# Power-attention layer on one core: who copies the weighted sums out of PSUM

## The chip, the cores and the metric

One program on one core of one Trainium2 chip. The metric is device time in microseconds (us) for one execution, from launch to end; a run's figure is the median of several executions. Engines are called by their profile names: PE (TensorE matmul), PEld (TensorE weight load), DVE (VectorE), ACT (ScalarE), POOL (GpSimd), SP (SyncE, which issues DMAs).

## The reference, cut to what matters

The program is a stack of four layers over x of 16 batches x 256 tokens x 128 channels, each with a layer norm before it, a layer norm after it and a residual sum: softmax attention, softmax attention with a mixture of experts, **power attention**, and a second mixture of experts with limited places. The change lies in the third:

```
q, k, v, gates = x @ W.T                       # 16 heads of 8 channels
log_G = cumsum(log_sigmoid(gates))             # decays
S = q k.T                                      # per head, 256 x 256
Z = 2*log(|S| + 1e-7) + log(scale) + log_G[t] - log_G[s],  s <= t only
P = exp(Z - rowmax(Z));  y = (P @ v) / sum(P)
x = x + layernorm(y)
```

exp of twice a logarithm is a square, so the kernel computes P as (|S| + 1e-7) squared times exp of the decays, without the maximum; numerator and denominator both come out of one product with V that has a column of ones.

## The kernel before, in words

The power layer (`power_layer`) works through 16 batches, called steps t. A step has 16 heads in 8 units u of two heads; n = 8t + u counts the units. Queries and keys are split in two halves of 128 tokens, so that each head has a near part (two diagonal blocks) and a far part (late queries against early keys). Each engine runs one hand-written loop over t and u, and the order in those loops is the order on the engine. For one unit:

- PE `near_blocks(n)` makes the decays (`decay_ps`, two buffers, line 1553) and the near scores (line 1557), one unit ahead; `far_scores(n)` (line 1571) the rest of the scores and so releases S. Ahead of the decays stands a mask matmul (line 1536); in steps below 10 one extra mask matmul, and in steps 14 and 15 two (line 1535), whose results are overwritten: filler.
- DVE takes |S| out of PSUM (line 1412, `AP`), a bit mask on integers, as the first work of its slot n.
- ACT makes exp of the decays (line 1232, `EP`) in slot n and the square of |S| (line 1220, `PTP`) of unit n - 1.
- POOL multiplies the two (line 991) in its slot n + 2.
- PE `times_v(t, g)` (line 1590) takes four heads (group g of 4) at once: 24 matmul records into one PSUM bank `pvP`, 384 columns. Its places are u = 6 of step t and u = 0, 2, 4 of step t + 1.
- `sums(t, g)` copies this bank to `OSP` in SBUF. The bank is single: `times_v` of the next group waits for the copy (`s_os`). The slots of the copies are u = 7 of step t and u = 1, 3, 4 of step t + 1; in slot 4 the product stands in the same unit of PE.
- In u = 5, 6, 7 of step t + 1 PE turns the sums (`turn_out`, line 1509, needs all four copies), and DVE divides them (`far_sums` L1330, `normalize_early`, `normalize_late` L1337).

S and |S| lock into each other: PE's `far_scores(n)` waits for |S| of n - 1, DVE's |S| of n waits for `far_scores(n)`; |S| has four buffers, freed by the squares. PE's mask matmul of n + 1 waits for ACT's exponential of n - 1.

Between these stand the small works of other batches. On ACT: `turned_in` (L1108, yT, slot 3; PE's projection L1468 of the same unit waits for it), `in_root` (slot 3), `out_root` (L1174 lvP and L1176 prsP, slot 4), `high` (L1112 HLP, slot 4; DVE's `low_parts` L1273 in slot 5 wait for it), `values` and `softplus` (slot 7; DVE's `log_gates` of slot 7 wait for them), and in slot 7 of steps 3, 6 and 9 rows of the layer before. On DVE: moments, decay rows, `far_keys` (slot 6), and guests of the layer before in steps 3, 6 and 9 (L2556 and others).

Of the kernel before, what the change touches and what calls it, by code (L numbers as in the profile page):

```python
# [36 lines left out]
ACT = mybir.ActivationFunctionType  # L37
# [3 lines left out]
P = 128  # L41
# [5 lines left out]
NG, NJ = 4, 4  # L47
# [783 lines left out]
def power_layer(nc, low, weighted_in, top, take, X, cst, cstb, QK, Vx, w, Y, chosen, router, bias, yd, wi, wo, gated, dram):  # L831
# [6 lines left out]
    UNITS = gated.UNITS  # L838
    with ExitStack() as ctx:
# [4 lines left out]
        def pb(name, banks):  # L844
            return ctx.enter_context(nc.psum_tensor(f"{name}P", [P, banks, 512], F32))

        def sem(name):
            return take(f"{name}P")
# [4 lines left out]
        pv_ps = pb("pv", 1)  # L853
# [20 lines left out]
        OS = sb("OS", [P, 2, 3, NG, P], F32)  # L874
# [18 lines left out]
        full = {n: sem(f"full_{n}") for n in POWER_A + POWER_B}  # L893
# [18 lines left out]
        s_pv = sem("s_pv")  # L912
        s_os = sem("s_os")
# [20 lines left out]
        def has(t):  # L934
            return 0 <= t < NB
# [29 lines left out]
        def reach(eng, sem, count):  # L965
            if count > 0:
                eng.wait_ge(sem, count)
# [180 lines left out]
        def scalar(act, guests):  # L1148
            def values(t):
                reach(act, full["V"], t + 1)  # L1150
                reach(act, free["V"], t)
                wide = bank("V").rearrange("p (c s) -> p c s", c=TC)
                act.activation(ge[:], wide[:, :, D:D + H], ACT.Abs).then_inc(s_ge, 1)
                reach(act, s_pv, NG * (t - 2))
                act.activation(Vx[:, t % 3, :, :, 0:DH], wide[:, :, 0:D].rearrange("p c (h d) -> p c h d", d=DH),
                               ACT.Copy).then_inc(s_ge, 1)

            def softplus(t):
                act.wait_ge(s_ge, 4 * t + 2)
                act.activation(ge[:], ge[:], ACT.Exp, scale=-1.0).then_inc(s_ge, 1)  # L1160
                act.wait_ge(s_ge, 4 * t + 3)
                act.activation(ge[:], ge[:], ACT.Ln, bias=1.0).then_inc(s_ge, 1)

            def in_root(t):
                act.wait_ge(s_ln, 4 * t + 4)
                reach(act, s_y, 2 * t)
                act.activation(lv[:, 0, :], mv[:, :, 1], ACT.Ln, bias=eps[:, 1:2]).then_inc(s_rs, 1)
                act.wait_ge(s_rs, 2 * t + 1)
                act.activation(rs[:], lv[:, 0, :], ACT.Exp, scale=-0.5).then_inc(s_rs, 1)

            def out_root(t):
                act.wait_ge(s_lp, 4 * t + 4)
                reach(act, s_tmp, 2 * t)
                act.activation(lv[:, 1, :], pmv[:, :, 1], ACT.Ln, bias=eps[:, 1:2]).then_inc(s_prs, 1)  # L1174
                act.wait_ge(s_prs, 2 * t + 1)
                act.activation(prs[:], lv[:, 1, :], ACT.Exp, scale=-0.5).then_inc(s_prs, 1)  # L1176

            def factors(t):
                reach(act, full["CS"], t + 1)
                reach(act, s_yn, t - 2)  # L1180
                act.activation(fac[:, t % 3, :, :], bank("CS")[:, S:S + 2 * H].rearrange("p (a h) -> p a h", a=2),
                               ACT.Exp).then_inc(s_fac, 1)

            def route_root(t):
                act.wait_ge(s_rl, 4 * t + 4)
                reach(act, s_Y, t)
                act.activation(rlv[:], rmv[:, :, 1], ACT.Ln, bias=eps[:, 1:2]).then_inc(s_rrs, 1)
                act.wait_ge(s_rrs, 2 * t + 1)
                act.activation(rrs[:], rlv[:], ACT.Exp, scale=-0.5).then_inc(s_rrs, 1)

            def route_norm(t):
                act.wait_ge(s_rnm, t + 1)
                for c in range(TC):
                    last = act.activation(Y[:, t * TC + c, :], batch_rows(t)[c], ACT.Identity, bias=rnm[:, c:c + 1],
                                          scale=rrs[:, c:c + 1])
                last.then_inc(s_Y, 1)

            def route_turned(t):
                act.wait_ge(full["RT"], t + 1)
                reach(act, full["RL"], t)  # L1200
                act.activation(YT[:], bank("RT")[:, 0:S], ACT.Copy).then_inc(free["RT"], 1)

            def odds():
                act.wait_ge(s_choose, 2)
                act.activation(chosen.ex[:, 0:EARLY, :], chosen.pr[:, 0:EARLY, :], ACT.Exp).then_inc(s_odds, 1)

            def second_odds():
                act.wait_ge(s_choose, 8)
                act.activation(chosen.gap[:, 0:EARLY], chosen.gap[:, 0:EARLY], ACT.Exp).then_inc(s_odds, 1)

            def square(n):
                act.wait_ge(s_abs, n + 1)
                reach(act, s_pv, (n - NW) // 2 + 1)
                if n == 5:
                    act.wait_ge(gated.s_up, UNITS)
                if n == 8:
                    gated.stores(act, 1)
                if n == 9:
                    act.wait_ge(gated.s_sum, 2 * gated.EARLY)
                act.activation(PT[:, n % NW, :], A[:, n % NA, :], ACT.Square, bias=eps[:, 0:1]).then_inc(s_sq, 1)  # L1220

            act.preload_act_table_set("natural_log_exp_and_others")
            act.wait_ge(s_zero, 3)
            for t in STEPS:
                for u in range(NU):
                    n = NU * t + u
                    if has(t):
                        act.wait_ge(s_decay, n + 1)
                        weighted(act, n - NE)
                        if n == 0:  # L1230
                            act.wait_ge(gated.s_prod, UNITS)
                        act.activation(E[:, n % NE, :], decay_ps[:, n % 2, :], ACT.Exp).then_inc(s_taken, 1)  # L1232
                    if 0 <= n - 1 < NU * NB:
                        square(n - 1)
                    if u == 4 and has(t - 2):
                        out_root(t - 2)
                    if u == 3 and has(t + 2):
                        turned_in(act, t + 2)
                    if u == 2 and t >= EARLY_CS - 1 and has(t + 1):
                        factors(t + 1)  # L1240
                    if u == 2 and t >= EARLY_CS - 1 and has(t + 1):
                        first_part(act, t + 1)
                    if u == 4 and has(t + 2):
                        high(act, t + 2)
                    if u == 3 and has(t + 3):
                        in_root(t + 3)
                    if u == 7 and has(t + 2):
                        values(t + 2)
                    if u == 7 and has(t + 2):
                        softplus(t + 2)  # L1250
                    for b in due("route_turned", t, u):
                        route_turned(b)
                    for b in due("route_root", t, u):
                        route_root(b)
                    for b in due("route_norm", t, u):
                        route_norm(b)
                    if t == NB and u == 5:
                        odds()
                    if t == NB + 1 and u == 5:
                        second_odds()  # L1260
                    guests.get((t, u), nobody)()
# [38 lines left out]
        def vector(dve, guests):  # L1300
            def log_gates(t):
# [1 line left out]
                reach(dve, full["CS"], t)  # L1303
                x = bank("V").rearrange("p (c s) -> p c s", c=TC)[:, :, D:D + H]
                dve.scalar_tensor_tensor(lg[:], x, 0.0, ge[:], ALU.min, ALU.subtract).then_inc(free["V"], 1)

            def sums(t, g):
                if t == 0 and g == 0:
                    dve.wait_ge(gated.s_down, UNITS)
                reach(dve, s_pv, NG * t + g + 1)  # L1310
                reach(dve, full["OT1"], t - 1)
                dve.tensor_copy(OS[:, t % 2, :, g, :], pv_ps[:, 0, 0:3 * P].rearrange("p (a s) -> p a s", a=3)).then_inc(s_os, 1)

            def far_keys(t):
                dve.wait_ge(s_fac, t + 1)
# [88 lines left out]
            for t in STEPS:  # L1404
                for u in range(NU):
                    n = NU * t + u
                    if has(t):
                        dve.wait_ge(s_S, n + 1)
                        reach(dve, s_sq, n - NA + 1)
                        if n == 3:  # L1410
                            dve.wait_ge(gated.s_down, UNITS)
                        dve.tensor_scalar(A[:, n % NA, :].bitcast(I32), score_ps[:, n % 2 * WU:n % 2 * WU + WU].bitcast(I32),  # L1412
                                          0x7FFFFFFF, None, ALU.bitwise_and).then_inc(s_abs, 1)
                    if u == 7 and has(t):
                        sums(t, 0)
                    if u == 1 and has(t - 1):
                        sums(t - 1, 1)
                    if u == 3 and has(t - 1):
                        sums(t - 1, 2)
                    if u == 4 and has(t - 1):  # L1420
                        sums(t - 1, 3)
                    if 0 <= n - 2 < NU * NB and (n - 2) % NU in MULT_BY_DVE:
                        multiply(dve, n - 2)
                    if u == 0 and has(t - 2):
# [1730 lines left out]
```

## Time and profile before

| | us |
|---|---|
| median of 3 runs (lowest, highest) | 1150.97 (1149.85, 1159.54) |
| the profiled execution | 1146.26 |
| its span, first to last instruction | 1144.5 |
| busy in the span: PE / DVE / ACT / POOL | 1006.8 / 880.9 / 767.3 / 692.8 |
| power layer, first to last step | 688.2 to 993.6 of the span |

Busy time is the time in which an engine had an instruction running; PE's ends are modelled, so its share says little. In the rows below a time in front of an engine's name is the start from the span's start; the next number is the duration of the instruction or of several merged ones; brackets at the end give the idle time of the engine in front and what ended it.

### The profile page before, as it was taken

The numbers are of one execution on the slowest core, as the hardware profiler recorded it, in microseconds if no ns is written. First come the engines' busy times: TensorE is split into PE (matmuls) and PEld (weight loads), VectorE is DVE, ScalarE is ACT, GpSimd is POOL, SyncE is SP. The second block draws the span as 40 slices with busy tenths as digits, with TensorE's granted clock in tenths as the row PEclk, the third lists the DMA queues.
The fourth block names the chain that finished last, engine by engine and source line by source line (L and its number), as shares of the span: only waits on it lengthen the run. The fifth ranks groups of instructions, "written<-read, shape, count | busy, mean of one in ns | idle before, by whom it ended". The sixth has DMA issues, their size and how long they took to land. (4 is left out here: it accounts for less than half of the span.)

```text
span 1144.5 us, 30966 instructions
## 1 busy us (share of the span) xinstructions
PE 1006.8 (88%) x10503; PEld 591.1 (52%) x10503; DVE 880.9 (77%) x2252; ACT 767.3 (67%) x1682; POOL 692.8 (61%) x814
## 2 busy tenths in 40 slices
PE   4899999999999977998999978989899999828975
PEld 2344444444444433457998854545455565524652
DVE  3899999999998996946657638989998999873323
ACT  1678888888888865873545646868687898743315
POOL 4244554566566538842776536878886887725763
PEclk9999999999999998989999988979897999957997
DMA  4112222211111111212534311112120112141227
GB/s 128 30 58 79 76 71 74 74 57 39 39 39 39 40 33 49 60 41 63 156 102 128 105 48 27 45 38 61 42 66 24 34 45 65 36 165 34 54 69 196
DMA packets 114423, 75.24 MB, mean 66 GB/s; under 512 B 21335, under 2 KB 107808, under 8 KB 114272
## 3 DMA queue, kind: packets, MB, share of 16 engines
q1 hardware_dynamic: 105840, 54.68, 17.5%
q0 software_dynamic: 7744, 18.13, 5.3%
q8 instruction: 90, 1.47, 0.5%
q14 instruction: 61, 0.50, 0.1%
q10 hardware_dynamic: 688, 0.46, 0.1%
HBM read 26.75 MB, written 26.51 MB: 47 GB/s over the span
## 5 line engine op out<-in xcount | busy, mean ns | idle before, releaser
L634 DVE TENSOR_REDUCE mxsS<-scoreS 128x2 f32<-128x512 f32 x512 | 327.4, 684 | 46.3 <-PE scoreS L776 42.5
L516 ACT ACTIVATE PTS<-stS 128x512 f32<-128x512 f32 x512 | 284.6, 596 | 62.0 <-PE stS L780 61.5
L776 PE MATMUL scoreS<-QK 31*128 31x256 f16 x1024 | 172.0, 280 | 29.0 <-DVE mxsS L634 16.5
L991 POOL TENSOR_TENSOR PTP<-PTP,EP 128x512 f32<-128x512 f32 x128 | 163.0, 1285 | 50.7 <-ACT PTP L1220 50.2
L780 PE MATMUL stS<-QK 32*128 32x256 f16 x1024 | 169.3, 277 | 1.3 <-ACT PTS L516 1.3
L698 PE MATMUL pvS<-PTS,Vx 128*32 128x256 f32 x2048 | 141.2, 394 | 0.3
L1220 ACT ACTIVATE PTP<-AP,epsP 128x768 f32<-128x768 f32 x128 | 119.1, 931 | 28.5 <-DVE AP L1412 28.2
L776 PEld LDWEIGHTS scoreS<-QK 31*128 31x128 f16 x1024 | 52.9, 93 | 151.0 <-DVE mxsS L634 104.4
L1412 DVE TENSOR_SCALAR AP<-score_psP 128x768 int32<-128x768 int32 x128 | 121.4, 949 | 12.3 <-PE score_psP L1571 11.3
L391 POOL TENSOR_TENSOR rsS<-veS,halfS 128x2 f32<-128x2 f32 (+1 forms) x32 | 33.1, 1035 | 134.4 <-DVE veS L602 67.9
L1232 ACT ACTIVATE EP<-decay_psP 128x512 f32<-128x512 f32 x128 | 75.8, 592 | 29.7 <-PE decay_psP L1553 28.4
L2170 POOL DMA_INDIRECT sorted<-gy,gidx x64 | 62.1, 971 | 37.2 <-DVE gowner L2511 18.6
L698 PEld LDWEIGHTS pvS<-PTS,Vx 128*32 128x32 f32 x2048 | 54.3, 111 | 50.3 <-issue 22.7
L2309 PE MATMUL gdown_ps<-down_w,gprod 128*128 (+1 forms) x496 | 65.7, 276 | 4.4 <-DVE XB L2545 4.4
L2309 PEld LDWEIGHTS gdown_ps<-down_w,gprod 128*128 128x128 f32 x496 | 60.3, 192 | 5.9 <-issue 4.9
L2599 DVE TENSOR_TENSOR gprod<-gsg,gup_ps 128x512 f32<-128x512 f32 x62 | 42.5, 686 | 21.7 <-PE gup_ps L2337 12.6
L2181 POOL DMA_INDIRECT ggot<-mixed,gidx x40 | 39.1, 977 | 32.8 <-DMA mixed<-gob 22.0
L1553 PEld LDWEIGHTS decay_psP<-MP 32*128 32x128 bf16 x512 | 29.6, 95 | 52.7 <-issue 48.2
L2358 ACT ACTIVATE ghTs<-gturn_ps,norm 128x256 f16<-128x256 f32 x46 | 21.7, 472 | 51.6 <-PE gturn_ps L2248 51.6
L780 PEld LDWEIGHTS stS<-QK 32*128 32x128 f16 x1024 | 52.2, 92 | 4.6 <-ACT PTS L516 2.4
L1571 PE MATMUL score_psP<-QK 31*128 31x128 f16 x256 | 37.1, 226 | 19.6 <-DVE AP L1412 19.0
L1557 PE MATMUL score_psP<-QK 31*128 31x128 f16 x512 | 52.5, 224 | 0.0
(397 smaller groups left out, 2415.6 us busy)
## 6 DMA issues: line engine op xcount, KB each, us to landing
QK<-HLS SPq DMA_DIRECT2D x384, 32.0 KB
QK<-HLP SPq DMA_DIRECT2D x192, 32.0 KB, 1.9
gsin<-sorted SPq DMA_DIRECT2D x46, 128.0 KB
mixed<-gob SPq DMA_DIRECT2D x46, 128.0 KB, 1.8
sorted<-ggot POOLq DMA_DIRECT2D x22, 256.0 KB, 2.6
expert_outputs<-tzero SPq DMA_DIRECT2D x8, 512.0 KB
cgot<-expert_outputs SPq DMA_DIRECT2D x16, 256.0 KB, 5.4
tokens<-XB SPq DMA_DIRECT2D x16, 128.0 KB, 3.0
```

The lines of the kernel that those rows point to most:

```text
L516: act.activation(PT[:, n % NPT, :], st_ps[:, (NS * t + n) % 3, :], ACT.Exp, scale=SCALE).then_inc(s_exp, 1)
L634: dve.tensor_reduce(mxs[:, u // 4, :, at], score_ps[:, n % 2, :].rearrange("p (c s) -> p c s", c=TC), AX.X, ALU.max).then_inc(s_max, 1)
L698: last = pe.matmul(pv_ps[32 * j:32 * j + 32, q], Vx[:, t % 3, c, 4 * g + j, :], PT[:, (4 * g + (j ^ 2)) % NPT, S * c:S * c + S], start=(c ...
L776: scored = pe.matmul(score_ps[:, k, cols], QK[part, new, g, 0, rows], QK[part, new, g, 1, :], start=True, stop=True)
L780: turned = pe.matmul(st_ps[:, (NS * t + n) % 3, cols], QK[part, old, g, 1, rows], QK[part, old, g, 0, :], start=True, stop=True)
L991: eng.tensor_tensor(w, w, E[:, n % NE, :], ALU.mult).then_inc(s_wd if n % NU in MULT_BY_DVE else s_wp, 1)
L1220: act.activation(PT[:, n % NW, :], A[:, n % NA, :], ACT.Square, bias=eps[:, 0:1]).then_inc(s_sq, 1)
L1232: act.activation(E[:, n % NE, :], decay_ps[:, n % 2, :], ACT.Exp).then_inc(s_taken, 1)
L1412: dve.tensor_scalar(A[:, n % NA, :].bitcast(I32), score_ps[:, n % 2 * WU:n % 2 * WU + WU].bitcast(I32), 0x7FFFFFFF, None, ALU.bitwise_and) ...
L1557: pe.matmul(score_ps[:, o:o + P], QK[band, t % 3, g, 1, rows], QK[band, t % 3, g, 0, rows], start=True, stop=True)
L2170: pool.indirect_dma_start(tables[h], bass.IndirectOffsetOnAxis(ap=idx[h][:, c, t:t + 1], axis=0), y[:, tiles[h].start + t, :], None).then_ ...
L2309: last = pe.matmul(down_ps[:, x % 2, t * D:(t + 1) * D], prod[:, x % NPROD, c * SLOTS + t * P:c * SLOTS + (t + 1) * P], down_flat[:, colum ...
```

## The change

The four copies of a step (`sums`) leave DVE's loop and enter ACT's loop, in slots of the same number. On DVE a copy stood right behind |S|; on ACT it stands behind the exponential and the square of the slot, ahead of `out_root`, `turned_in`, `high`, `values` and `softplus`. Waits and the count of `s_os` are the same; the instruction is an activation with the function Copy.

```diff
@@ scalar(act): new @@
+            def sums(t, g):
+                if t == 0 and g == 0:
+                    act.wait_ge(gated.s_down, UNITS)
+                reach(act, s_pv, NG * t + g + 1)
+                reach(act, full["OT1"], t - 1)
+                act.activation(OS[:, t % 2, :, g, :], pv_ps[:, 0, 0:3 * P].rearrange("p (a s) -> p a s", a=3), ACT.Copy)\
+                   .then_inc(s_os, 1)
...
                     if 0 <= n - 1 < NU * NB:
                         square(n - 1)
+                    if u == 7 and has(t):
+                        sums(t, 0)
+                    if u == 1 and has(t - 1):
+                        sums(t - 1, 1)
+                    if u == 3 and has(t - 1):
+                        sums(t - 1, 2)
+                    if u == 4 and has(t - 1):
+                        sums(t - 1, 3)
                     if u == 4 and has(t - 2):
                         out_root(t - 2)
                     if u == 3 and has(t + 2):
                         turned_in(act, t + 2)
@@ vector(dve, guests): taken out @@
-            def sums(t, g):
-                if t == 0 and g == 0:
-                    dve.wait_ge(gated.s_down, UNITS)
-                reach(dve, s_pv, NG * t + g + 1)
-                reach(dve, full["OT1"], t - 1)
-                dve.tensor_copy(OS[:, t % 2, :, g, :], pv_ps[:, 0, 0:3 * P].rearrange("p (a s) -> p a s", a=3)).then_inc(s_os, 1)
...
-                    if u == 7 and has(t):
-                        sums(t, 0)
-                    if u == 1 and has(t - 1):
-                        sums(t - 1, 1)
-                    if u == 3 and has(t - 1):
-                        sums(t - 1, 2)
-                    if u == 4 and has(t - 1):
-                        sums(t - 1, 3)
```

## Rows read from the trace of the kernel before

**Rows 1.** Busy windows: whole stage; columns are stretch, length, engines' busy us, clock
```profile
688.22:993.60 305.38, 284.02 (x3486) 159.22 (x3484) 277.65 (x625) 239.89 (x501) 242.49 (x223) 0.93 0.17 43
```
**Rows 2.** The same by step: 3, 4, 5, 6, 8, then 10 to 13 together, 11
```profile
743.87:770.40 26.53, 21.82 (x223) 11.30 (x222) 23.14 (x56) 15.44 (x34) 18.45 (x18) 0.74 0.13 34
770.40:789.35 18.95, 18.07 (x229) 10.11 (x229) 18.07 (x40) 16.69 (x38) 17.26 (x17) 1.00 0.24 58
789.35:808.00 18.65, 17.96 (x229) 10.10 (x228) 17.81 (x39) 15.29 (x34) 16.97 (x17) 1.00 0.22 58
808.00:832.11 24.11, 19.99 (x229) 10.89 (x228) 23.03 (x57) 15.59 (x35) 18.46 (x18) 0.86 0.17 43
851.05:873.04 21.99, 20.62 (x229) 11.27 (x228) 17.93 (x40) 15.65 (x34) 15.67 (x15) 0.84 0.17 41
895.62:960.85 65.23, 64.55 (x883) 40.00 (x883) 61.54 (x150) 61.33 (x135) 55.17 (x51) 1.00 0.17 46
912.23:928.27 16.04, 15.94 (x221) 9.95 (x220) 15.31 (x39) 15.13 (x35) 14.13 (x15) 1.00 0.14 35
```
**Rows 3.** Waits, stage and its tail: who waited for whom, total us, times, longest
```profile
PE score_psP L1571 <- DVE AP L1412: 19.0, 20, 3.9
DVE OSP L1312 <- PE pvP L1590: 11.2, 15, 2.0
```
**Rows 4.** Timeline of PE: first and last of the five longest such waits
```profile
704.61 0.28 PE L1571 MATMUL score_psP<-QK 31*128 31x128 f16 x2 [3.87 <-DVE AP L1412]
...
878.59 0.28 PE L1571 MATMUL score_psP<-QK 31*128 31x128 f16 x2 [0.74 <-DVE AP L1412]
```
**Rows 5.** Waits in steps 10 to 13
```profile
PEld score_psP L1571 <- DVE AP L1412: 3.1, 10, 0.6
...
ACT EP L1232 <- PE decay_psP L1553: 1.5, 3, 0.6
ACT lvP L1167 <- DVE mvP L1269: 1.4, 3, 0.7
```
**Rows 6.** Instruction groups of the stage: busy us, mean ns, idle before and releaser
```profile
L1312 DVE COPY OSP<-pvP 128x384 f32<-128x384 f32 x64 | 35.1, 548 | 12.0 <-PE pvP L1590 11.2 <-DVE pr L161 0.8
```
**Rows 7.** Instruction groups of ACT, same columns
```profile
L1232 ACT ACTIVATE EP<-decay_psP 128x512 f32<-128x512 f32 x128 | 75.8, 592 | 29.7 <-PE decay_psP L1553 28.4 <-POOL PTP L991 1.0
L1108 ACT ACTIVATE yTP<-misc_aP 128x256 f32<-128x256 f32 x14 | 5.2, 369 | 0.0
```
**Rows 8.** Timeline of ACT in step 11, slots 3 and 4
```profile
918.78 0.37 ACT L1108 ACTIVATE yTP<-misc_aP 128x256 f32<-128x256 f32 x1
...
921.74 0.28 ACT L1174 ACTIVATE lvP<-pmvP,epsP 128x2 f32<-128x2 f32 x1
...
922.16 0.58 ACT L1112 ACTIVATE HLP<-misc_aP 128x512 f16<-128x512 f32 x1
922.64 0.59 ACT L1232 ACTIVATE EP<-decay_psP 128x512 f32<-128x512 f32 x1
```
**Rows 9.** Timeline of PE in step 11, same slots
```profile
919.39 0.70 PE L1468 MATMUL misc_aP<-yTP,wq 128*128 128x256 f32 x2
...
921.78 0.40 PE L1590 MATMUL pvP<-PTP,VkP 128*32 128x128 f32 x8
```
**Rows 10.** Timeline of DVE in step 11, the copy of slot 4
```profile
922.25 0.56 DVE L1312 COPY OSP<-pvP 128x384 f32<-128x384 f32 x1 [0.45 <-PE pvP L1590]
```
**Rows 11.** Waits in steps 4 and 5
```profile
PEld score_psP L1571 <- DVE AP L1412: 2.8, 8, 0.4
...
PEld score_psP L1571 <- issue: 1.6, 8, 0.2
```
**Rows 12.** Timeline of DVE in step 6: the copy of slot 4
```profile
824.25 0.56 DVE L1312 COPY OSP<-pvP 128x384 f32<-128x384 f32 x1 [0.71 <-PE pvP L1590]
```
**Rows 13.** Timeline of PE in step 6: the scores of unit 6
```profile
827.13 0.28 PE L1571 MATMUL score_psP<-QK 31*128 31x128 f16 x2 [1.28 <-DVE AP L1412]
```
**Rows 14.** DVE's normalize line: count, then min/median/max ns, first and last start
```profile
L1337 DVE TENSOR_TENSOR ynP<-farP,rcP x16: 291/680/3061, 727.2 to 1002.7; 128x128 f32<-128x128 f32 x16
```

## The prediction

> **What bounds the kernel now.** The page's busy shares, in the table above, show no engine but PE near full over the whole program, and PE's share is no limit by itself, since its ends are modelled. So I cut out the one stage that the change touches. Its sixteen steps take 305 us; DVE is busy 278 of them, ACT 240 [rows 1], and DVE looks like the bound. By steps (a stretch runs from the first |S| of a batch on DVE to that of the next) there are three kinds [rows 2]. Steps 4 and 5 (2 and 7 are their like) take 18.95 and 18.65 us at full clock, PE busy 18. Steps 10 to 13, without the filler matmul, take 65.2 us or 16.3 each; in step 11 PE, DVE and ACT are all within 0.9 of the length. Steps 3, 6 and 8 (9 is their like) take 22 to 26.5 with the granted clock at 0.74 to 0.86 on average: partly 1.2 instead of 2.4 GHz.
>
> Who waits for whom decides whether DVE is the bound. PE's score matmuls wait 19.0 us for |S| in the whole stage, in 20 places [rows 3]. The five longest, in time order 3.87, 3.66, 2.84, 1.37 and 0.74 (first and last in [rows 4]), make 12.5 of it. One lies in step 0 behind DVE's guest work, four in steps 3, 6, 8 and 9 behind DVE's slot 0, in which no copy of sums stands. In steps 10 to 13 all waits of PE's weight loads for |S| are 3.1 us, 0.8 a step [rows 5]. So DVE is nearly full, yet frees PE in time: S, |S| and the next S go at PE's pace, and each DVE slot has only to fit into one PE unit.
>
> **The change part by part.** *Off DVE:* 64 copies of 0.548 us, 35.1 us, and the 11.2 us that DVE idles in front of them for the product with V [rows 6, 3]. *Onto ACT:* 64 copies of 128x384 out of PSUM. No ACT instruction of that shape is in the trace; its neighbours take 0.369 us (128x256) and 0.592 (128x512), both PSUM to SBUF [rows 7], so 0.48 by interpolation, with those two as bounds. Back to back ACT overlaps by 0.10: HLP starts at 922.16 and takes 0.58, its follower starts at 922.64 [rows 8]. So a copy occupies ACT for 0.38 us (0.27 to 0.49), 1.5 us a step.
>
> *The wait that moves with it.* Three of the four slots mostly find the product done; the copy in slot 4 doesn't, and DVE idles 0.45 us for it in step 11 [rows 10]. On ACT it stands behind the square that ends by 921.74 and ahead of lv/prs and HLP [rows 8]. The product with V ends at 921.78+0.40=922.18 [rows 9]: ACT would sit about 0.45 us. It becomes a little more. The copy of slot 3 is now ahead of yT, which ends at 918.78+0.37=919.15 [rows 8]; PE's projection starts 0.24 later [rows 9] and stands ahead of the product in PE's queue, so 0.38 more before yT makes it 0.1 to 0.3 late when ACT has no slack. I take 0.55 for the wait, bounds 0.3 and 0.8. Queued behind it on ACT are prs, HLP and the exponentials of the decays; DVE's low parts wait for HLP, PE's mask matmuls for the exponentials.
>
> *Steps 10 to 13.* ACT is busy 61.3 of 65.2 us [rows 2]. Add 16 copies of 0.38 (6.1) and four waits of 0.55 (2.2): 69.6. The 3.9 us that ACT idles now are mostly 1.5 for decays and 1.4 for moments [rows 5]; both end because ACT arrives later, so they are filled first. ACT becomes the bound, 69.6 against 65.2; of the 4.4 some 0.4 are absorbed by PE being one unit ahead at the end: **+4.0**. Bounds: +2 (no wait, all idle filled) and +8 (the idle stays).
>
> *Steps 2, 4, 5, 7.* PE's floor is close: in steps 4 and 5 its weight loads wait 2.8 us for |S| in 8 places, but a usual pause there is 1.6/8=0.2 [rows 11], so 0.6 a step is over. Of that the copies make a part, above all the one in slot 1, which delays |S| 2 and 3: 0.3 a step comes back. Against it stands ACT. In step 5 it is busy 15.29 of 18.65 [rows 2], and 1.5+0.55 fit, though HLP comes some 0.8 later and takes back what DVE gained in slot 4. In step 4 it is busy 16.69 of 18.95, with rows of the layer before; 16.69+1.5+0.55=18.74 leaves nothing, and yT and HLP make PE wait. I take -0.3 for steps 2 and 5, +0.4 for 4 and 7: **+0.2**; bounds -2 (all of the 0.6 comes back, less a little) and +3 (0.8 lost in each).
>
> *Steps 3, 6, 9.* In slot 4 of step 6 DVE does the copy after a wait of 0.71 [rows 12], then guest moments, then |S| 5, and PE waits 1.28 us for that |S| [rows 13]. Wait and copy, 0.71+0.55, leave DVE's path: -1.1 in each of three steps. But ACT enters the next step (4, 7, 10) with as much work on a shorter time, and gives back about 0.8 each: **-0.9** together; bounds -4 and 0. The stall of slot 0 has no copy in it and stays, and with it the low clock.
>
> *Steps 0, 1, 8, 14, 15 and the tail:* PE is the bound there (at the low clock, or with two fillers); ACT has idle time there, and in the tail it is mostly waiting. That idle time hides the copies; without it they would cost up to 1.5 us a step in steps 14 and 15: **-0.1**.
>
> Sum: 4.0+0.2-0.9-0.1 = **+3.2 us** on the profiled execution's 1146.26 (1144.5 span and 1.8 around it): 1149.5. The runs shown lie at 1149.85 to 1159.54 with a median of 1150.97, 4.7 above the profiled one. The time asked for is such a median, so 1150.97+3.2: **1154**. A measurement of this kernel tells 1% (11.5 us) from no change.
>
> **The rivals.** *DVE is the bound.* For: 278 of 305 us busy, the fullest of DVE, ACT and POOL; a full removal would be 35.1+11.2=46 us less, 1105 [rows 1, 3, 6]. Against: PE hardly waits. Of the 19.0 us of PE's waits 19.0-12.5=6.5 lie outside the five stalls [rows 3, 4]: -6.5, **1144.5**, chance 0.13; the full 46 us get 0.02. The Trainium skill, page Perfetto Trace Analysis, section Identifying Performance Opportunities, says to relieve the engine with the highest occupancy and not to trust TensorE's matmul busy share. By that rule the change gains, towards this rival's 1105, where the sum by waits loses 3.2 us. The trace agrees only as far as the occupancy goes, 278 us against 240; its waits speak the other way.
>
> *The clock falls less.* For: DVE's normalize instruction on two SBUF operands takes 0.29 to 3.06 us for one shape [rows 14], and the longest stands in step 8, while POOL multiplies back to back; with squares coming later from ACT the multiplies separate, DVE gets in between, and the falls in steps 8 and 9 go. Each costs about 3 us (step 8: 21.99 against 18.65 of step 5 [rows 2]). Two fewer, with some slot 0 time: -9, **1145**, chance 0.12. Against: POOL has a backlog in slot 0, so a square 0.8 later is still in time. The Trainium skill's page SBUF — State Buffer, section Who interferes with whom, describes an exclusive lock between VectorE and GpSimd for operations with two SBUF inputs; the 0.29 to 3.06 us agree with it.
>
> *ACT is the bound everywhere* (slower). Mechanism: the wait in slot 4 blocks HLP and the exponentials in steps with a filler too, DVE's low parts and PE's decays wait on ACT, and PE loses 0.8 to 1 us in each of steps 2 to 9 as well. It decides from the point where ACT's busy time, copies and wait exceed the step: 18.74 against 18.95 in step 4. Price 8x0.9+4.0, with nothing gained in 3, 6, 9: +11, **1162**; new idle stretches of PE could add a clock fall of 3 us. Chance 0.16.
>
> That the change doesn't do what it says: the copies are plainly ACT's in the diff; 0.02, then 1151.
>
> **How the numbers follow.** Forecast 0.55, around 1154 from 1148 to 1160; DVE bound 0.15; clock 0.12; ACT everywhere 0.16; no change 0.02. The range takes in the bounds of the sum and reaches past the middles of the moderate rivals on both sides, which leaves out some 0.2: 1142 to 1164. Faster by over 1% (below 1139.5): the full DVE case, and part of the two moderate ones if they come together, 0.07. Slower by over 1% (above 1162.5): the upper half of ACT everywhere and a little of the forecast, 0.11. The rest, 0.82, lies within.
>
> **What would show it.** Right: steps 10 to 13 at about 17.1 us each with ACT busy over 16.5 and DVE about 13.5; ACT idle before the slot-4 copy for V's product by about 0.5 us in each step; PE's projection or decays waiting for ACT where nothing waits now; steps 3 and 6 still with a fallen clock; DVE idle several us more in total. The copy at 0.45 to 0.50 us. Wrong: steps 10 to 13 as short as before (then ACT's idle holds more than I think), steps 4, 5, 7 below 18 us (then PE did wait on DVE), or a changed count of stretches at half clock, which moves the time by 3 us each and which no sum of busy times foresees.

## The result and the profile after

The changed kernel takes 1169.63 us (median of 4 runs, 1166.56 to 1172.84) beside 1150.41 for the kernel before (4 runs, 1145.11 to 1159.54): a ratio of **1.0162, 95% interval 1.0110 to 1.0214**. It is slower, and lies above the predicted range. The profiled execution took 1171.17 us (span 1169.3). The ratios here and below leave out executions more than 1.5% above the fastest of the same kernel.

First the busy windows of the changed kernel, with the columns of [rows 1, 2]: the whole stage, steps 1, 3, 4, 6, 7, 9, 10, and 11 to 13 together; then three short stretches.

```profile
691.90:1016.71 324.81, 296.08 (x3484) 164.59 (x3482) 260.88 (x565) 258.51 (x562) 242.09 (x223) 0.89 0.16 41
711.62:730.84 19.22, 17.94 (x213) 9.71 (x209) 15.97 (x33) 15.38 (x34) 14.05 (x13) 0.90 0.10 25
749.71:773.35 23.64, 19.34 (x223) 10.23 (x222) 21.50 (x53) 15.78 (x35) 17.63 (x17) 0.86 0.15 40
773.35:795.90 22.55, 20.95 (x229) 11.45 (x228) 17.30 (x37) 18.20 (x42) 18.05 (x18) 0.85 0.20 47
814.68:838.25 23.57, 20.10 (x229) 10.84 (x228) 21.49 (x53) 16.78 (x38) 17.62 (x17) 0.86 0.18 46
838.26:860.81 22.55, 20.95 (x229) 11.44 (x228) 17.31 (x37) 18.20 (x42) 18.04 (x18) 0.85 0.20 48
883.69:907.35 23.66, 22.07 (x230) 11.69 (x230) 19.72 (x53) 16.79 (x38) 14.53 (x14) 0.78 0.10 26
907.35:932.29 24.94, 23.17 (x221) 13.62 (x220) 15.25 (x36) 18.27 (x43) 16.06 (x16) 0.66 0.11 30
932.29:983.96 51.67, 48.71 (x663) 30.09 (x663) 42.10 (x98) 48.57 (x110) 39.87 (x37) 1.00 0.16 43
774.90:780.50 5.60, 4.12 (x44) 2.17 (x36) 5.57 (x13) 5.04 (x10) 5.19 (x5) 1.00 0.50 114
780.50:787.30 6.80, 6.80 (x53) 3.53 (x52) 3.94 (x10) 4.97 (x13) 5.36 (x6) 0.50 0.05 12
913.60:930.70 17.10, 17.10 (x147) 9.79 (x145) 9.12 (x19) 10.49 (x24) 10.82 (x11) 0.50 0.07 17
```

The same windows of the kernel before, as far as the rows ahead don't have them: steps 1, 7, 9, 10, then 11 to 13, and the part of step 4 that answers to 774.90:780.50.

```profile
707.80:725.67 17.87, 17.87 (x217) 9.84 (x214) 16.38 (x37) 14.54 (x30) 14.39 (x13) 0.89 0.09 23
832.11:851.05 18.94, 18.07 (x229) 10.10 (x229) 18.07 (x40) 16.70 (x38) 17.25 (x17) 1.00 0.23 58
873.04:895.62 22.58, 20.56 (x228) 11.32 (x227) 20.70 (x56) 15.63 (x34) 14.56 (x15) 0.85 0.10 27
895.62:912.23 16.61, 16.23 (x221) 10.02 (x220) 15.95 (x41) 15.66 (x36) 12.98 (x12) 1.00 0.14 37
912.23:960.85 48.62, 48.32 (x663) 29.98 (x663) 45.59 (x111) 45.67 (x100) 42.18 (x40) 1.00 0.18 49
771.95:777.55 5.60, 5.28 (x76) 3.06 (x70) 5.57 (x15) 4.47 (x10) 5.00 (x5) 1.00 0.47 111
```

The stage is 324.81-305.38=19.4 us longer. The stage also starts 3.7 us later, which no edit explains (its start scatters from 685.6 to 691.9 over the kernels of this study), and the rest is behind it. Read the clock column against [rows 2]. Steps 4 and 7 ran at 1.00 (2.4 GHz); now they hold a stretch at 0.50 (1.2 GHz) and take 22.55 us each, +3.60 and +3.61. Step 10 has a stretch of 17.1 us at 0.50 and goes from 16.61 to 24.94, +8.3. These three make 15.5 of the 19.4. Steps 11 to 13 stay at full clock and take 51.67 instead of 48.62, +3.05. Each kernel has one trace, while the mean clock differs from execution to execution (0.921 to 0.931 in the four of the changed kernel); so the steps are read from one pair of traces, and the verdicts further down go by the times of many executions.

The windows of 5.60 us show what came ahead of the fall: in this stretch of step 4 PE was busy 5.28 us before and 4.12 after, and then the clock falls for 6.8 us. Length times one minus the clock estimates what a stretch loses: 305.38x0.07=21.4 us before, 324.81x0.11=35.7 after. So some 14 of the 19.4 us are clock (1.6 either way, from the rounding of each clock), and the work at full clock grew by about 5.

Who makes PE idle in step 4 is in its timeline (changed kernel; in brackets the idle time before, and its releaser):

```profile
776.05 0.39 PE L1536 MATMUL decay_psP<-cstb 128*128 128x512 bf16 x1 [0.52 <-ACT EP L1240]
...
778.91 0.58 PE L1522 MATMUL misc_aP<-router,YTP 128*128 128x8 f32 x4 [0.62 <-ACT YTP L1209]
779.83 0.28 PE L1572 MATMUL score_psP<-QK 31*128 31x128 f16 x2 [0.34 <-DVE AP L1421]
```

Twice the profile names ACT: the exponential of the decays and the turned rows of the route (YT) are late. The third wait is DVE's, whose normalize row of slot 0 now meets POOL's multiplication (775.47 to 776.75). It is shown as it was in the kernel before, and as it is now, with the |S| that PE waits for:

```profile
771.90 0.49 DVE L1337 TENSOR_TENSOR ynP<-farP,rcP 128x128 f32<-128x128 f32 x1
```
```profile
774.83 2.08 DVE L1346 TENSOR_TENSOR ynP<-farP,rcP 128x128 f32<-128x128 f32 x1
...
778.82 0.96 DVE L1421 TENSOR_SCALAR AP<-score_psP 128x768 int32<-128x768 int32 x1
```

DVE was busy without a gap up to this |S|, and PE's scores start as it ends. Had YT come in time, PE would have stood for |S| all the same: of the 1.48 us in step 4 only the first 0.52 are ACT's by the wait that ends last, the other 0.96 are DVE's. Step 7 repeats this (0.52, 0.63 and 0.33). Step 10 has 0.41, 0.52 and 0.84 us for ACT and none for DVE there.

The copies, and ACT's exponentials (groups of the stage; a few records are missing):

```profile
L1240 ACT ACTIVATE EP<-decay_psP 128x512 f32<-128x512 f32 x127 | 75.1, 591 | 9.5 <-PE decay_psP L1554 8.2 <-POOL PTP L991 1.0
L1189 ACT ACTIVATE OSP<-pvP 128x384 f32<-128x384 f32 x61 | 29.8, 488 | 30.1 <-PE pvP L1591 30.1
```

A copy takes 0.488 us. ACT used to idle 29.7 us in front of its exponentials [rows 7]; that was its lead over PE. Now it idles 9.5 there and 30.1 in front of the copies, with the exponentials behind. Slot 4 of step 11 and of step 10, on ACT:

```profile
941.29 0.93 ACT L1228 ACTIVATE PTP<-AP,epsP 128x768 f32<-128x768 f32 x1
942.65 0.49 ACT L1189 ACTIVATE OSP<-pvP 128x384 f32<-128x384 f32 x1 [0.43 <-PE pvP L1591]
...
943.94 0.59 ACT L1240 ACTIVATE EP<-decay_psP 128x512 f32<-128x512 f32 x1
...
923.17 0.49 ACT L1189 ACTIVATE OSP<-pvP 128x384 f32<-128x384 f32 x1 [3.34 <-PE pvP L1591]
```

In steps in which no fall begins (1, 2, 5 and 11 to 15) this wait is 0.42 to 1.24 us; in step 11 it is 0.43. In step 10, inside the stretch at 0.50, PE reaches the product late and ACT stands 3.34 us for it; in steps 4, 7, 8 and 9, in a low stretch or right behind it, 2.5 to 3.3. So in these steps the low clock comes with a longer wait, and the wait stands ahead of what PE needs next.

### The profile page after: what moved, and what is told of

Read it like the earlier page. It is cut to its first block and busy times, and to the rows that moved or that the text cites. A ratio compares the mean times of both kernels' runs of the same rounds, so it can differ in the third digit from the quotient of the medians.

```text
span 1169.3 us, 30967 instructions
## 1 busy us (share of the span) xinstructions
PE 1024.0 (88%) x10503; PEld 599.9 (51%) x10503; DVE 862.5 (74%) x2188; ACT 788.7 (67%) x1746; POOL 694.0 (59%) x814
## 3 DMA queue, kind: packets, MB, share of 16 engines
q1 hardware_dynamic: 105840, 54.68, 17.2%
## 5 line engine op out<-in xcount | busy, mean ns | idle before, releaser
L1228 ACT ACTIVATE PTP<-AP,epsP 128x768 f32<-128x768 f32 x128 | 119.4, 933 | 21.6 <-DVE AP L1421 21.4
L1537 PE MATMUL decay_psP<-cstb 128*128 128x512 bf16 x128 | 53.6, 419 | 1.5 <-ACT EP L1240 1.5
L1189 ACT ACTIVATE OSP<-pvP 128x384 f32<-128x384 f32 x64 | 31.3, 489 | 34.6 <-PE pvP L1591 34.6
```

The lines of the kernel that those rows point to most:

```text
L1537: pe.matmul(decay_ps[:, n % 2, :], cstb[:, 0:P], late, start=True, stop=False)
```

## The experiments

The theories that the expectations name: **A**, the copies of slots 7 and 1 behind the guest's rows on ACT; **B**, ACT is too full, and every copy costs the same; **C**, the copy of slot 4 (or 3 and 4), which waits ahead of ACT's small works and exponentials; **D**, late squares push POOL's multiplications onto DVE's instruction of slot 0; **E**, PE is stopped by ACT directly; **F**, the three slot-4 copies of steps 3, 6 and 9. All ratios are to the kernel before, timed beside it; brackets are 95% intervals. A split keeps the deleted copy on DVE for the slots that the test leaves there.

**Which slots.** In these a test goes in front of each call; `g` is the slot's number (0 to 3 for slots 7, 1, 3, 4):

```diff
+        def on_act(t, g):
+            return g in (0, 1)            # slots71;  g in (2, 3): slots34;  g == 3: s4only
-                    if u == 4 and has(t - 1):
+                    if u == 4 and has(t - 1) and on_act(t - 1, 3):
                         sums(t - 1, 3)
```

> The copies of slots 7 and 1 are ACT's, those of slots 3 and 4 stay DVE's. Theory A (two copies in slots 7 and 1, behind the guest rows that ACT does in slot 7 of steps 3, 6 and 9, make ACT late in units 0 and 1 of steps 4, 7 and 10; PE waits there and its clock falls): the three steps stay near 22.5, 22.5 and over 20 us with a mean clock under 0.9, ratio to before 1.008 to 1.015. Theory B (ACT is simply too full, each copy costs the same wherever it stands): half of the change's loss, 1.008, spread over all steps. Theory C (the wait in slot 4 does it): 1.000 to 1.002, no new stretch at the low clock.

> The copies of slots 3 and 4 are ACT's, those of slots 7 and 1 stay DVE's. A: steps 4 and 7 stay at full clock and near 19 us, steps 11 to 13 at 16.5 to 17; ratio 1.000 to 1.004. B: 1.008. C: most of the loss, 1.012 to 1.016, with the clock falling in steps 4, 7 and 10.

> Only the copy of slot 4 on ACT, the other three on DVE as before. It is the one that sits waiting for V's product ahead of the exponentials. If that wait is what counts (theory C in its narrow form): most of the loss of the two copies of slots 3 and 4 together (1.0145), so 1.009 to 1.014. If the copy of slot 3 ahead of yT counts as much, or both only add up to the lateness that moves POOL: 1.000 to 1.006.

Slots 7 and 1 alone: 1.0038 [1.0002, 1.0073]. Slots 3 and 4: 1.0145 [1.0088, 1.0202]. Slot 4 alone: **1.0193 [1.0131, 1.0254]**. One of the four copies carries the whole loss, so B falls. In the profile of slot 4 alone, steps 4, 7 and 10 are long with a fallen clock as in the changed kernel:

```profile
771.84:796.99 25.15, 21.33 (x229) 11.47 (x229) 20.43 (x39) 17.07 (x39) 17.73 (x18) 0.80 0.18 43
839.43:863.37 23.94, 20.14 (x229) 10.85 (x229) 20.42 (x38) 17.06 (x39) 17.74 (x18) 0.86 0.18 45
909.46:931.48 22.02, 20.66 (x221) 12.16 (x220) 16.62 (x39) 16.72 (x39) 14.49 (x15) 0.77 0.11 28
```

But PE's waits there are not those of the changed kernel. In step 4 PE waits 0.15 and 0.25 us for ACT and then 3.29 for an |S| that DVE holds back behind its normalize row (step 7: 3.28, behind a row of 3.31):

```profile
773.33 3.33 DVE L1359 TENSOR_TENSOR ynP<-farP,rcP 128x128 f32<-128x128 f32 x1
```
```profile
780.55 0.39 PE L1593 MATMUL score_psP<-QK 31*128 31x128 f16 x2 [3.29 <-DVE AP L1434]
```

POOL multiplies meanwhile (774.00 to 776.50). So with this copy alone PE's waits in steps 4 and 7 are mostly those of D, and only in step 10 those of E (0.52 and 0.47 us for ACT). Nor do these three steps mark the loss by themselves: they are long in the one trace of `slots71` too (21.64, 21.65 and 22.00 us), whose time is within 0.4% of the kernel before.

**Sparing the guest's steps.** All on ACT but slot 7 of steps 3, 6 and 9 and slot 1 of the step behind: the same test with `(t, g) not in ((3, 0), (3, 1), (6, 0), (6, 1), (9, 0), (9, 1))`.

> As the changed kernel, but six copies stay DVE's: slot 7 of steps 3, 6 and 9, and slot 1 of the steps after them. A: the falls of the clock in steps 4, 7 and 10 are gone, these take about 19, 19 and 17.5 us, steps 11 to 13 still 17.1 to 17.3; ratio 1.002 to 1.006. B and C: 58 of 64 copies are still ACT's, so 1.013 to 1.016.

1.0190 [1.0137, 1.0243], no better than the change. A falls.

**The order on ACT.** All four calls go behind the small works of their slot (yT, lv/prs, the high parts, softplus, the route's rows); `s4late` does so with the copy of slot 4 alone on ACT:

```diff
-                    if u == 4 and has(t - 1):
-                        sums(t - 1, 3)
                     if u == 4 and has(t - 2):
                         out_root(t - 2)
...
                     for b in due("route_norm", t, u):
                         route_norm(b)
+                    if u == 4 and has(t - 1):
+                        sums(t - 1, 3)
```

> All four copies are ACT's in the same slots, but behind the slot's small works (yT, HLP, softplus, the turned route rows) instead of ahead of them. A: PE gets the turned route rows of unit 1 earlier, but the exponential of unit 0 is as late as in the change, so falls in steps 4, 7 and 10 become fewer but not all go; 1.005 to 1.012. B: as the change, 1.014 to 1.018. C: HLP and yT no longer wait for the product with V, so most of the loss is gone, 1.000 to 1.004.

> Only the copy of slot 4 on ACT, and behind the slot's small works (lv/prs, the high parts) instead of ahead of them: those run while V's product is still on its way, and the copy finds it done. If ACT's standing for the product is what makes the squares late: the loss of 1.0193 goes to 1.000 to 1.005. If it is that DVE no longer stands there and PE runs ahead, or the copy's 0.4 us on ACT: 1.010 to 1.018.

All four late: 1.0030 [0.9994, 1.0067]. Slot 4 late: **0.9999 [0.9966, 1.0032]**, against 1.0193 ahead of the same works. Copy, engine and what DVE is relieved of are the same; only the order differs, and the loss is gone. The times say so, not the traces: those of `late` and `s4late` are of long executions (1158.95, median 1157.80; 1158.49, median 1150.94), and steps 4, 7 and 10 have falls in them too. Step 4 of `s4late`:

```profile
769.40:798.13 28.73, 25.47 (x229) 13.50 (x228) 19.43 (x39) 17.43 (x39) 19.52 (x19) 0.64 0.16 45
```

Slot 4 of step 12 on ACT, at full clock, first in `s4only`, then in `s4late`:

```profile
956.93 0.92 ACT L1234 ACTIVATE PTP<-AP,epsP 128x768 f32<-128x768 f32 x1
958.33 0.49 ACT L1195 ACTIVATE OSP<-pvP 128x384 f32<-128x384 f32 x1 [0.47 <-PE pvP L1612]
...
959.14 0.58 ACT L1118 ACTIVATE HLP<-misc_aP 128x512 f16<-128x512 f32 x1
959.62 0.59 ACT L1246 ACTIVATE EP<-decay_psP 128x512 f32<-128x512 f32 x1
```

```profile
949.47 0.93 ACT L1234 ACTIVATE PTP<-AP,epsP 128x768 f32<-128x768 f32 x1
...
950.72 0.58 ACT L1118 ACTIVATE HLP<-misc_aP 128x512 f16<-128x512 f32 x1
951.20 0.48 ACT L1195 ACTIVATE OSP<-pvP 128x384 f32<-128x384 f32 x1
951.57 0.60 ACT L1246 ACTIVATE EP<-decay_psP 128x512 f32<-128x512 f32 x1
```

From the end of the square to the exponential: 959.62-957.85=1.77 us, and 951.57-950.40=1.17. In the kernel before it is 922.64-921.84=0.80 [rows 8 and the line below], in the changed kernel 943.94-942.22=1.72. Late, the copy finds its product done, because the high parts ran while it was on its way. The square of the kernel before:

```profile
920.91 0.93 ACT L1220 ACTIVATE PTP<-AP,epsP 128x768 f32<-128x768 f32 x1
```

**Wait or release?** ACT's wait for the product added to the kernel before, in slot 4 of every step (`wait_all`) or of steps 3, 6 and 9 (`wait_only`), all copies on DVE; and DVE's copy moved behind |S| of slot 5, ACT untouched (`dve_slot5`):

```diff
+                    if u == 4 and has(t - 1):          # wait_only: t in (3, 6, 9)
+                        reach(act, s_pv, NG * t)
                     if u == 4 and has(t - 2):
                         out_root(t - 2)
```
```diff
-                    if u == 4 and has(t - 1):          # dve_slot5, in DVE's loop
+                    if u == 5 and has(t - 1):
                         sums(t - 1, 3)
```

> The kernel before, all copies on DVE, with only ACT's wait for V's product added in slot 4 of every step. If the wait is enough: 1.010 to 1.018. If it needs DVE's release at the same place, as with the wait in steps 3, 6 and 9 alone (0.9995): 0.999 to 1.004.

> The kernel before, all copies on DVE, and only the wait of ACT added: in slot 4 of steps 3, 6 and 9 ACT waits for V's product before it goes on, as it would for a copy. If ACT's wait in front of the exponentials is the cause by itself: 1.008 to 1.018. If it takes DVE's release too (with DVE standing at the same place, PE does not run ahead and ACT has the 1.3 us after the product to catch up): 0.999 to 1.004.

> The kernel before, with DVE's copy of slot 4 moved behind |S| of slot 5, still on DVE: DVE's wait for V's product goes, and ACT gets nothing to do. If the release of DVE by itself is the cause, since PE then runs ahead of ACT: 1.005 to 1.015. If ACT's wait is needed: PE's waits of about 1.1 to 1.3 us in steps 3, 6 and 9 go and nothing takes their place, 0.992 to 1.000.

The wait alone in all steps: 1.0030 [0.9994, 1.0066]; in three steps: 0.9995 [0.9969, 1.0020]. DVE's release alone: 1.0049 [1.0013, 1.0086], though not cleanly, for PE's transposes now wait for the moved copy (1.24 us in step 3 of its profile). Neither gives 1.6%, nor do both together by addition. `s4late` has DVE's release and the copy's time on ACT, but no wait ahead of the small works, and loses nothing (0.9999). So the wait is needed, but not enough by itself; whether the release or the copy's time ahead of the small works has to go with it was not run. A reading that fits, though argued and not shown: in the kernel before DVE stands at the same product, holds |S| back there, and so PE can't run ahead of an ACT that waits.

**The three copies of steps 3, 6 and 9.** The test of the first group with `(t, g) in ((2, 3), (5, 3), (8, 3))`, the product's own `t` being one less (`only369`), and with `not in` (`guard369`).

> The kernel before with three of the 64 copies on ACT: those of slot 4 in steps 3, 6 and 9. In these steps DVE used to stand 0.7 us for V's product and hold back |S| 5 by the copy and the guest's moments. Theory F (with DVE let go, units 5 to 7 run ahead while ACT waits for the product in front of the exponentials; the guest's rows keep ACT from catching up, the squares and POOL's multiplications enter the next step 1 us late, DVE's additions of slot 0 collide with them, PE idles and the clock falls in steps 4, 7 and 10): 1.009 to 1.019 of the kernel before, from three instructions. If the lateness is piled up over all steps by every slot-4 copy: 0.999 to 1.004.

> All copies on ACT but these three, which DVE keeps. Theory F: steps 4, 7 and 10 without their new clock falls, or with one of three, and what is left is the 1 us each of steps 10 to 13: 1.002 to 1.007 of the kernel before. If every slot-4 copy counts: 1.012 to 1.017.

These three alone: 1.0057 [1.0026, 1.0088]. All but them: 1.0169 [1.0112, 1.0227]. F falls as the sole cause. In the profile of `guard369` step 4 is whole again, and the clock falls in steps 5, 7 and 10 (and in others):

```profile
772.78:791.88 19.10, 18.05 (x229) 10.18 (x229) 15.48 (x35) 17.63 (x41) 16.57 (x16) 1.00 0.21 56
791.88:813.58 21.70, 20.78 (x229) 11.35 (x228) 16.41 (x35) 16.68 (x38) 17.09 (x17) 0.84 0.21 49
838.24:860.08 21.84, 20.90 (x229) 11.29 (x229) 15.48 (x36) 17.75 (x41) 16.59 (x16) 0.84 0.19 50
908.69:931.43 22.74, 20.99 (x229) 12.45 (x228) 14.66 (x35) 17.84 (x42) 13.28 (x13) 0.77 0.10 27
```

**The clock.** More filler matmuls in the changed kernel, in the units where PE idled:

```diff
+    MORE = [(t, u) for t in (4, 7, 10) for u in (0, 1, 2)]
-                for _ in range(AGAIN if t >= NB - 2 else t < 10):
+                for _ in range(AGAIN if t >= NB - 2 else 3 if (t, u) in MORE else t < 10):
```

> The changed kernel with two more filler matmuls in each of units 0 to 2 of steps 4 and 7, and three in those of step 10 (0.2 us each at full clock, 4.5 us in all if none of it lies in an idle gap). If the loss is the clock that falls after the idle gaps of PE there: the falls in steps 4, 7 and 10 go, those steps come down to 19 to 20 us, and the time is 1.003 to 1.010 of the kernel before. If the loss is the waiting itself and the low clock would do no harm without it: the fillers come on top, 1.016 to 1.021.

1.0045 [1.0002, 1.0087] instead of 1.0162: work added, time saved. Steps 4, 7 and 10 of its profile:

```profile
776.51:795.28 18.77, 18.64 (x233) 10.49 (x233) 15.02 (x36) 17.19 (x40) 14.71 (x15) 1.00 0.16 44
842.22:861.52 19.30, 18.82 (x233) 10.55 (x232) 16.82 (x36) 17.70 (x41) 17.73 (x17) 1.00 0.22 56
906.94:925.35 18.41, 17.84 (x235) 10.66 (x234) 14.89 (x36) 17.54 (x41) 14.26 (x14) 1.00 0.12 32
```

All three at full clock: 18.77, 19.30 and 18.41 us with two or three fillers more in each of three units. ACT carries the same work as in the changed kernel; PE, slowed by the fillers, hardly waits for it there (0.23 and 0.34 us in step 10), and the clock stays. It isn't a clean test of E in step 4, for DVE's normalize row takes 0.29 us there and not 2.08. And this execution, at 1164.14 us the longest of five (median 1156.85), has falls elsewhere, in steps 3, 5 and 8 above all (27.64, 23.11 and 24.12 us). Step 3:

```profile
748.87:776.51 27.64, 24.63 (x225) 13.02 (x224) 21.03 (x52) 16.72 (x37) 18.20 (x17) 0.69 0.14 35
```

What the clock cost can be estimated over all executions, as the record has the span and the mean granted clock of each: span times one minus the clock, as a mean of the executions that the ratios use. It is 66.4 to 70.1 us in four series of the kernel before, timed beside the tests, 85.0 in the changed kernel, 86.8 with the copy of slot 4 alone, 69.5 with that copy late and 67.9 with the fillers. The rest of the span is 1078.6 to 1080.3 us before, 1082.9 in the changed kernel and 1081.6 with the copy of slot 4 alone. So most of the loss of these two was the clock's.

What sets off a fall isn't shown. Here is step 4 of `slots71`, a stretch and the one right behind it, and the same stretch of step 4 in `guard369`:

```profile
770.90:776.50 5.60, 4.81 (x58) 2.57 (x48) 4.45 (x14) 5.39 (x12) 3.97 (x5) 1.00 0.41 109
776.50:783.30 6.80, 6.80 (x51) 3.26 (x52) 4.49 (x11) 4.68 (x12) 6.19 (x6) 0.50 0.07 18
```
```profile
774.41:780.01 5.60, 4.80 (x58) 2.56 (x46) 4.44 (x14) 5.39 (x12) 3.97 (x5) 1.00 0.39 107
```

PE waits 0.17 and 0.63 us for ACT in both; the clock falls behind the first and stays at 1.00 behind the second. Short waits go ahead of the falls, but they don't bring one each time.

**The collision in slot 0.** The far sums are added in place in PSUM, and the normalize row has one operand there (the semaphores `s_far` and `free["OT1"]` take over):

```diff
-                dve.tensor_tensor(far[:], turned("OT1", t)[:, :, 0:DH + 1], far[:], ALU.add).then_inc(free["OT1"], 1)
+                dve.tensor_tensor(turned("OT1", t)[:, :, 0:DH + 1], turned("OT1", t)[:, :, 0:DH + 1], far[:], ALU.add)\
+                   .then_inc(s_far, 1)
-                divide(t, 1, far[:], s_yn)
+                divide(t, 1, turned("OT1", t), free["OT1"])
```

> The changed kernel with one edit: the far sums of slot 0 are added in place in PSUM, so that DVE's normalize multiplication has one operand in PSUM instead of two in SBUF. Theory D (the loss runs through POOL: ACT's squares come later, POOL's multiplications slide onto DVE's two-SBUF-operand multiplication in slot 0 of a step, which then takes 2.1 us in step 4 instead of 0.5; PE waits and the clock falls): that row falls to about 0.3 us in every step, slot 0 of steps 4 and 7 is 1 us shorter or more, at least two of the new clock falls go, 1.003 to 1.009 of the kernel before. Theory E (PE is stopped by ACT directly, by late exponentials and late yT, and the collision only happens beside it): slot 0 shrinks on DVE, PE's falls stay, 1.013 to 1.017.

> The kernel before with the same in-place addition in PSUM. Theory D: the stalls of slot 0 in steps 8 and 9, where that multiplication takes up to 3.06 us, shrink as well and one or two of the clock falls go: 0.985 to 0.997. Theory E, or if the guest's own instructions of slot 0 simply take the collision over: 0.998 to 1.002.

> All four copies on ACT behind the small works of their slots, and the far sums added in place in PSUM. If the two effects add up (1.0030 and the 0.9939 of the addition alone): 0.994 to 0.999, no better than the kernel before with the addition alone. If ACT in the better order lets DVE use what the addition frees: 0.986 to 0.992, the best version so far.

In the changed kernel: 1.0136 [1.0106, 1.0167]. In the kernel before: **0.9939 [0.9903, 0.9975]**. With all copies late on ACT: 0.9954 [0.9927, 0.9981]. The group of DVE's normalize rows, first of the kernel before, then of the changed kernel, then of the changed kernel with this edit:

```profile
L1337 DVE TENSOR_TENSOR ynP<-farP,rcP 128x128 f32<-128x128 f32 x14 | 15.6, 1112 | 0.5
```
```profile
L1346 DVE TENSOR_TENSOR ynP<-farP,rcP 128x128 f32<-128x128 f32 x14 | 20.5, 1466 | 0.5
```
```profile
L1346 DVE TENSOR_TENSOR ynP<-misc_bP,rcP 128x128 f32<-128x128 f32 x29 | 8.4, 291 | 1.0
```

The row costs 0.291 us wherever it stands. The Trainium skill, page SBUF — State Buffer, section Who interferes with whom, has an instruction of VectorE with two SBUF inputs contend with one of GpSimd that reads SBUF, and one with at most one (outside the two-port modes) not; these rows agree. The edit takes 0.6% off the kernel before. Off the changed one it takes nothing that can be told from no change (1.0136 beside 1.0162, with overlapping intervals), and the two with the edit lie 1.0136/0.9939=1.020 apart: the collision of this row is real, and the changed kernel's loss doesn't need it. In its trace (1154.98 us, the shortest of six, median 1161.66) PE waits 0.52 and 0.63 us for ACT in steps 4 and 7 as before, but not for DVE behind them, and both steps take 20.64 us, with the clock at 0.92 and 1.00; step 10 keeps its waits for ACT and its 24.93 us at 0.66. So E holds in step 10, and in steps 4 and 7 both play. `s4only`, where D is the larger part of the waits, was not run with this edit. Both kernels are beaten by `before_far`; the copies on ACT, in their better order, add nothing to it (0.9954).

## Why the prediction was wrong, step by step

**What bounds the kernel** was right as far as the copies go: taking them off DVE gained nothing, neither two of the slots (1.0038) nor all four with the better order on ACT (1.0030). The rivals with DVE as the bound (1144.5, 1105) fall with that. The list of PE's "five longest" waits is wrong, though (so is the title of [rows 4]): two of 1.28 us and one of 1.05, in steps 6, 9 and 3 behind the copy of slot 4, are longer than the 0.74. And DVE's slot 0, which holds no copy, does bind: its normalize row was worth 0.6% (`before_far`).

**The copy** was 0.48 us by interpolation, measured 0.488. **The wait in slot 4** was 0.55 us, measured 0.43 in step 11. For the whole stage the same number would make 9 us; ACT idled 30.1 in front of the copies, most of it in or behind low stretches. The square before it ends at 921.84 and not by 921.74, which is small beside that.

**Steps 10 to 13** were +4.0, as 17.1 us a step. Steps 11 to 13 came as forecast: 51.67/3=17.2 each, +3.05, with ACT at 16.2 busy (over 16.5 was the sign) and DVE at 14.0 (about 13.5). Step 10 did not: +8.3, with 17.1 us at the low clock, for which the sum has no term.

**Steps 2, 4, 5, 7, the failed step.** The prediction says: "In step 4 it is busy 16.69 of 18.95 [...] leaves nothing, and yT and HLP make PE wait. I take [...] +0.4 for 4 and 7". That ACT without slack makes PE wait holds in part: PE waited for the exponential and YT rather than yT and HLP, and behind them for an |S| of DVE's that the term doesn't have. The size is wrong. Measured: +3.60 and +3.61; steps 2 and 5 have +0.67 and +0.12 where -0.3 each was forecast. The waits were priced as their own length, 0.4 us a step. They were 1.48 us, and behind them 6.8 us ran at 1.2 GHz, some 3.4 us lost. With fillers the same steps take 18.77 and 19.30 us at full clock. The upper bound (0.8 us lost in each) left the clock out as well.

**Steps 3, 6, 9** were -0.9 with bounds -4 and 0. Measured -2.9, -0.5 and +1.1 [rows 2 and the windows above], -2.35 in all. That this lies within the bounds is in part luck: the clock went from 0.74 to 0.86 in step 3 and from 0.85 to 0.78 in step 9, and neither is in the term. What DVE's release should take away is gone, PE's waits of 1.05, 1.28 and 1.28 us behind the copy of slot 4; the waits of slot 0 grew by 0.6 to 0.7 each. What ACT gives back in 4, 7 and 10, 0.8 us each, was far too low.

**The other steps** were -0.1. Measured: +2.4 in all. Step 1 has +1.35 (19.22 against 17.87) at nearly the same clock: PE waits 1.23 us there for ACT's exponential at 726.05, so the idle time of ACT that was to hide the copy and its wait did not. Step 8 has +0.9 (22.88 against 21.99).

**The rivals.** "ACT is the bound everywhere" (1162) named the cause: the wait in slot 4 ahead of the exponentials. Its 0.8 to 1 us in each of steps 2 to 9 did not come that way (steps 2 and 5: +0.67 and +0.12). It allowed for a new clock fall of 3 us; there were three places, and the last cost 8.3. "The clock falls less" is wrong in sign: the squares come later, and the normalize row collides more, 1466 ns on average instead of 1112. The closing part did name "a changed count of stretches at half clock" as what no sum of busy times foresees; the range gave it no room above.

**What stays open.** ACT's wait alone, DVE's release alone and the three guest steps alone give 0.3, 0.5 and 0.6%; together, with the copy, 1.9%, most of it clock. How the late ACT reaches PE was not settled: directly (E), or by POOL and DVE's normalize row (D), which makes the long waits of `s4only`. Nor was it why the clock falls in just these steps: it moves to others when one place is mended (`guard369`, `after_fill`), and the same waits bring a fall in one trace and none in another.

## What to carry to other kernels

A copy that waits goes behind what the engine can do meanwhile: one copy a step ahead of ACT's small works cost 1.9% here, behind them nothing that could be measured, and which engine carries it made no difference that could be measured. Where PE's clock can fall, price each new wait of PE not by its length alone but also by the stretch at the low clock that may follow it, and give the range room for several; a wait on an engine with 12% to spare (ACT in step 4) isn't free if it eats that engine's lead over PE. To find a cause, change the order alone and keep the work: `s4only` and `s4late` differ by one place in a queue. And don't take one trace for the kernel: ask whether the profiled execution is a typical one, and use the clock of every execution where the record has it.

## What the chip showed that was not expected

In `slots71` PE was busy 4.81 of 5.60 us with no wait longer than 0.63 us, and the granted clock fell to 0.50 right behind it; with 4.80 of 5.60 and the same waits in `guard369` it stayed at 1.00. Fillers of PE paid for themselves: 21 added matmuls of 128x512 brought the ratio from 1.0162 to 1.0045. And three instructions of 64, moved to another engine, made the program 0.57% slower.
